# Softmax denominators of a head pair: four products of 32 array columns instead of four of 64, with small VectorE copies behind them

## The reference, cut to what matters

```python
q, k, v = tanh(states @ Wq + bq), tanh(states @ Wk + bk), tanh(states @ Wv + bv)   # 16 heads x 64
alpha = einsum('bhqd,bhkd->bhqk', q, k) / sqrt(64)
alpha = where(causal, alpha, finfo.min)
alpha = softmax(alpha, axis=-1)
ctx   = einsum('bhqk,bhkd->bhqd', alpha, v)
return tanh(ctx @ Wo + bo)
```

## Time and profile before

| | before |
|---|---|
| median of 3 runs | 1678.64 us (1678.16 to 1680.62) |
| span of the profiled execution | 1681.5 us |
| PE busy | 1618.6 us (96%) |
| DVE busy | 1440.7 us (86%) |
| ACT busy | 1208.0 us (72%) |
| POOL busy | 460.7 us (27%) |
| chain that ended last | PE 85%, DVE 8%, ACT 3%, issue 2%, POOL 1% |
| line 608 in that chain | 3% |
| granted PE clock over the span | 0.989 |

### The profile page before, as it was taken

One profiled execution on the slowest core, in us unless ns is written; L12 is line 12 of the kernel. 1 busy time (PEld: TensorE's weight loads), 2 busy tenths in 40 slices (PEclk: granted clock), 3 DMA queues, 4 the chain that ended last, 5 costly groups with the idle time before them and its releaser, 6 DMA issues.

```text
span 1681.5 us, 38177 instructions
## 1 busy us (share of the span) xinstructions
PE 1618.6 (96%) x14842; PEld 712.2 (42%) x14842; DVE 1440.7 (86%) x2099; ACT 1208.0 (72%) x1208; POOL 460.7 (27%) x563
## 2 busy tenths in 40 slices
PE   7899999999999999998999999999999999989996
PEld 3444444444444444444233333333332332456774
DVE  6877777888888888996999999999999999488888
ACT  5666766666667666654887888788878888775776
POOL 4211112333332323341234232323332332220004
PEclk9999999999999999997999999999999999999998
DMA  5311111011110110011012000200030000000001
GB/s 142 72 39 37 37 37 39 20 37 37 37 37 36 37 37 21 22 32 32 14 39 51 9 12 16 48 12 13 16 74 20 13 16 21 1 8 8 14 13 50
DMA packets 46602, 52.94 MB, mean 31 GB/s; under 512 B 9279, under 2 KB 33551, under 8 KB 46482
## 3 DMA queue, kind: packets, MB, share of 16 engines
q1 hardware_dynamic: 45584, 50.05, 10.2%
q10 hardware_dynamic: 898, 1.22, 0.3%
HBM read 15.07 MB, written 10.49 MB: 15 GB/s over the span
## 4 chain that ended last, share of the span: by engine, by line
PE 85%; DVE 8%; ACT 3%; issue 2%; POOL 1%; ACTq 0%; POOLq 0%; DVEq 0%
PE psum L1872 15%; PE psum L590 15%; PE psum L571 11%; PE psum L1857 9%; PE psum L1883 7%; PE psum L533 5%; PE psum L1503 4%; PE psum L1470 4%; PE psum L608 3%; DVE arena L2333 3%; PE psum L628 2%; PE psum L553 1%; ACT arena L2101 1%; PE psum L554 1%; PE psum L555 1%
## 5 line engine op out<-in xcount | busy, mean ns | idle before, releaser
L2333 DVE TENSOR_REDUCE arena<-psum 128x2 f32<-128x1024 f32 x490 | 585.4, 1219 | 39.2 <-PE psum L1883 33.0
L2101 ACT ACTIVATE arena<-psum 128x1024 f32<-128x1024 f32 x512 | 524.2, 1026 | 131.6 <-PE psum L1857 117.9
L755 ACT ACTIVATE arena<-psum 128x2048 f32<-128x2048 f32 (+1 forms) x160 | 274.0, 1713 | 229.0 <-PE psum L571 228.9
L1872 PE MATMUL psum<-arena 128*32 128x256 f32 x4096 | 327.8, 392 | 0.7
L859 POOL TENSOR_SCALAR_AFFINE_SELECT arena<-arena 128x512 f32<-128x512 f32 (+1 forms) x160 | 152.5, 971 | 508.9 <-ACT arena L755 508.9
L590 PE MATMUL psum<-arena,hs 128*64 128x512 f32 (+3 forms) x1536 | 283.0, 496 | 0.2 <-POOL arena L859 0.2
L571 PE MATMUL psum<-arena 64*128 64x512 f16 (+3 forms) x2304 | 215.0, 324 | 2.1 <-DVE arena L907 1.6
L1857 PE MATMUL psum<-arena 32*128 32x512 bf16 x1024 | 198.9, 385 | 3.7 <-DVE arena L2333 3.0
L1883 PE MATMUL psum<-arena 32*128 32x512 bf16 x980 | 189.0, 382 | 6.0 <-ACT arena L2101 2.4
L907 DVE TENSOR_TENSOR arena<-arena 128x1024 f16<-128x1024 f32 x64 | 78.4, 1226 | 101.5 <-ACT arena L734 101.5
L590 PEld LDWEIGHTS psum<-arena,hs 128*64 128x64 f32 x1536 | 96.0, 136 | 141.5 <-issue 125.2
(11 more groups left out here) (221 smaller groups left out, 2127.5 us busy)
## 6 DMA issues: line engine op xcount, KB each, us to landing
arena<-arena SPq DMA_DIRECT2D x30, 512.0 KB, 2.9
arena<-arena SPq DMA_DIRECT2D x46, 128.0 KB, 2.2
arena<-latent_q SPq DMA_DIRECT2D x64, 64.0 KB, 2.0
arena<-latent_k SPq DMA_DIRECT2D x64, 64.0 KB, 2.0
arena<-arena SPq DMA_DIRECT2D x60, 64.0 KB, 2.3
X<-in_L_attn_states SPq DMA_DIRECT2D x4, 512.0 KB, 4.6
latent_q<-arena SPq DMA_DIRECT2D x16, 96.0 KB, 2.2
latent_k<-arena SPq DMA_DIRECT2D x16, 96.0 KB, 2.3
```

Of the source, the lines that this page charges most:

```text
L755: nc.scalar.activation(probs[g], SC[:, :, 0:WIDTH[g]], ACT.Exp, scale=DH ** -0.5).then_inc(exp_done, 1)
L1872: last = nc.tensor.matmul(OT[ROWS * c:ROWS * (c + 1), h * HALF // 2:(h + 1) * HALF // 2], v_cols[par][:, kt, 2 * pr + i, :], e_probs[u % 4 ...
L2101: nc.scalar.activation(e_probs[u % 4], src, ACT.Exp, scale=KD ** -0.5).then_inc(e_done, 1)
L2333: nc.vector.tensor_reduce(half_tops[:, kh, qt, 2 * pr:2 * pr + 2], src.rearrange("p (i c) -> p i c", i=2), AX.X, ALU.max).then_inc(top_don ...
```

## The change

The four products of a pair now have 32 columns of ones each and go to four groups of 32 rows of one PSUM bank: row group c holds head c // 2 and half c % 2 of the queries. They raise `den_done` once, by 2. DVE transposes that one bank with one instruction; `denT` has 512 words instead of 1024. The reciprocal reads the 16 numbers of each partition twice and writes 32. Four new copies (`share`), each of 32 partitions by 16 numbers, take the inverses of a row group to the neighbouring row group of the same head, so that all 64 rows of a head hold both halves; then `spread` is as before. `share` stands where `spread` stood, between the first and the second `hi_third`, and `spread` moves behind the second. In the tail `share` stands directly ahead of `spread`.

```diff
-        denT = a1b.take(S)
+        denT = a1b.take(HALF)
...
+        QB = HALF // 32
+        INVERSE = 6
...
-                for half in range(2):
-                    now = slice(half * HALF, (half + 1) * HALF)
-                    for s in range(2):
-                        last = nc.tensor.matmul(PJ[s * DH:(s + 1) * DH, now], ones, sums[par][:, s, now],
-                                                start=True, stop=True, skip_group_check=True)
-                    last.then_inc(den_done, 1)
+                for c in range(4):
+                    s, half = c // 2, c % 2
+                    last = nc.tensor.matmul(PJ[ROWS * c:ROWS * (c + 1), 0:HALF], ones[:, 0:ROWS],
+                                            sums[par][:, s, half * HALF:(half + 1) * HALF],
+                                            start=True, stop=True, skip_group_check=True)
+                last.then_inc(den_done, 2)
...
-                for half in range(2):
-                    dve.wait_ge(den_done, 2 * n + half + 1)
-                    now = slice(half * HALF, (half + 1) * HALF)
-                    nc.vector.transpose(denT[:, now], PJ[:, now]).then_inc(den_read, 1)
+                dve.wait_ge(den_done, 2 * n + 2)
+                nc.vector.transpose(denT, PJ[:, 0:HALF]).then_inc(den_read, 2)
...
-                nc.vector.reciprocal(rden_col, denT.rearrange("p (b c) -> p b c", c=32)[:, :, 0]).then_inc(rden_ready, 1)
+                v = denT.rearrange("p (b c) -> p b c", c=32)[:, :, 0].unsqueeze(1).to_broadcast([P, 2, QB])
+                nc.vector.reciprocal(rden_col.rearrange("p (h b) -> p h b", h=2), v).then_inc(rden_ready, 1)
+
+            def share(n):
+
+                dve.wait_ge(rden_ready, INVERSE * n + 1)
+                for c in range(4):
+                    half, other = c % 2, c ^ 1
+                    now = slice(half * QB, (half + 1) * QB)
+                    nc.vector.tensor_copy(rden_col[ROWS * other:ROWS * (other + 1), now], rden_col[ROWS * c:ROWS * (c + 1), now]
+                                          ).then_inc(rden_ready, 1)
...
                 hi_third(i, par, 0)
                 if at_least(i, 1):
+                    share(i - 1)
+                hi_third(i, par, 1)
+                if at_least(i, 1):
                     spread(i - 1)
-                hi_third(i, par, 1)
                 hi_third(i, par, 2)
```

## The result

| | before | changed |
|---|---|---|
| median, same chip, 4 runs each | 1678.46 us (1678.16 to 1680.62) | 1697.57 us (1697.40 to 1697.97) |
| ratio, 95% interval | | 1.0100 (1.0082 to 1.0117) |
| span of the profiled execution | 1681.5 us | 1696.1 us |
| granted PE clock over the span | 0.989 | 0.986 |
| chain that ended last | PE 85%, DVE 8%, issue 2% | PE 72%, DVE 13%, issue 9% |

The account below looks back on a forecast made before the run. PE and DVE's chain were taken to set the pace together, with POOL's selects limiting PE. Terms +8.8 (21 late pairs), -1.9 (pairs 2 to 9), +0.4 (pair 1) and +0.1 gave +7.4, 1686.0 us; range 1674 to 1690.

Parts of the forecast that it names:

- PE's block: Denominator products on PE: two rounds 0.92 us plus 0.20 for arrangement changes, 1.12 instead of 1.82, saving 0.70.
- Rival 3: PE alone counts: its 0.70 us arrives in full in 31 pairs, -22 us, 1656.6 us; chance 0.02.
- rival 4: The four products don't run side by side: block 1.92 us, PE +0.1 a pair, 1686 to 1690 us; chance 0.03.
- Rival 2: One charge absent: copies one at a time but unblocked by the select, or flowing but blocked; 1675.6 us; chance 0.31.
- Rival 1: Copies cheap, 0.36 us for four, and the select lets them pass; about 11 us faster, 1667.6 us; chance 0.08.
- pair 14's kind: Pairs 10 to 27 and 28 to 30, closing on DVE's chain: +0.42 us each, +8.8 us over 21 pairs.
- (a): DVE's transposes of the denominators: one goes, -0.60 us in pair 14 and -0.74 in pair 7.
- Step (e): Second and third `hi_third` on DVE, now with the transpose between them: -0.10 us.
- the 0.68: Four DVE copies that change rows, each beginning when the one before has ended; part of 2.20 us from first to second `hi_third`.
- the charge of the select: First DVE copy waits for POOL's select of group 4: 0.31 to 0.48 us, taken as 0.36.
- Pair 7's kind: Pairs 2 to 9, where PE itself is last before the values: -0.24 us each, -1.9 us over eight.
- the last pair and the product behind the loop: End of the loop, where DVE waits for the products too: +0.1 us.

Follow-up runs that it names:

- the narrow products alone: Changed kernel with PE's four 32-column products, but two DVE transposes of the one bank, the old order and no copies; 1676.75 us, ratio 0.9987 to the kernel before.
- the short select: Changed kernel with POOL's select of group 4 cut from 128 columns to 8; 1685.88 us, ratio 1.0022 to the kernel before.

## Why the prediction was wrong

**Right: the mechanism of the pairs and its place.** PE's block (1.00 us and 0.10 ahead of it, against 1.12), PE waiting ahead of context 3 and ahead of the values, DVE's chain setting the late pairs, copies one at a time, a select blocking the first: each is in the rows, and each was taken away by itself, with the pairs going where the mechanism says. Rival 3 is refuted by the narrow products alone, rival 4 by the block of 1.00 us. Rival 2 needed one of the two charges to be absent; they are there with 0.49 (row changes) and 0.32 us (select). Rival 1 needed both to be absent. No kernel here has the copies on DVE with both charges gone; with the copies gone altogether a late pair gains 22.43 - 22.16 = 0.27, where rival 1 had 0.3.

**Off by 3 us: sizes.** In pair 14's kind the transpose gives the -0.60 of (a): 367.89 - 366.88 = 1.01 to the first `hi_third`, where it was 365.95 - 364.34 = 1.61. Step (e) gives its -0.10: from the second `hi_third` to line 922 it is 372.53 - 370.19 = 2.34, against 1.15 for the transpose and 369.47 - 368.18 = 1.29. The mis-sized term is the middle one, 2.30 instead of 2.20, because each held instruction (four copies and the `hi_third` behind them) starts some 0.03 us after the end of the one before it, which the 0.68 left out; the charge of the select, 0.32 for 0.36, gives a part of that back. So +0.52 by these rows and +0.51 by the windows, not +0.42. Pair 7's kind gained 0.06 instead of 0.24: the same 0.10, and the transpose starts 0.14 us behind the end of the products (206.50 + 1.07), so that step (a) gives -0.62, not -0.74. DVE and PE there:

```profile
207.71 0.72 DVE L927 STREAM_TRANSPOSE arena<-psum 128x512 f32<-128x512 f32 x1 [0.16 <-PE psum L609]
...
213.37 1.21 DVE L922 TENSOR_TENSOR acc<-psum,acc 128x1024 f32<-128x1024 f32 x1
```
```profile
214.63 0.23 PE L555 MATMUL psum<-arena 128*128 128x128 f16 x1 [0.37 <-DVE acc L922]
```

Over the program: pairs 10 to 30 +10.3, not +8.8; pairs 1 to 9 +0.2, not -1.9 and +0.4; the lead, where no instruction changed, +0.7; and about -1.0 behind the loop at the high clock. That makes the +10.2 of equal clocks out of the forecast's +7.4. The lead up to the first pair lasts between 24.5 and 26.1 us over the kernels of this study; what sets it is open.

**The failed step: "the last pair and the product behind the loop ... +0.1 by the same terms".** The terms were DVE's and PE's durations at full clock. At full clock they were nearly right: in the execution with the high clock the changed kernel is 11.2 us behind ahead of the last pair and 11.1 at the start of the last denominators. They put the clock at nothing without a reason: that PE has two long waits there, that the clock stood at half behind both, and that the change lengthens both. The low clock cost 1.6 us in this very stretch and 9.4 in all, 3.4 times the error in all other terms together (2.8). The same blindness is in the base line. The trace of the kernel before already had its clock at half in this place:

```profile
783.00:790.00 7.00, 7.00 (x34) 4.49 (x31) 2.62 (x8) 2.05 (x2) 0.00 (x0) 0.50 0.29 61
```

The profile's 0.989 stood in the table of before, and read as "2.9 above the median" it hid that this kernel has executions with and without 5 us of low clock. The range up to 1690 contained the kernel at the high clock (1688.54) and nothing else of it.

**Open.** Waits of 1.98 and 3.24 us were followed by 23.9 us at half clock in one execution and by full clock, but for a few us, in the next. That filling PE's waits makes the low clock rarer is shown for the changed kernel (four of four runs at 0.991 to 0.994, against one of eight above 0.989 without) and for the one with the copies on ACT (0.991 to 0.993, against 0.987 to 0.990). That the length of the waits orders the kernels is not shown: with the copies on ACT the waits are 1.17 and 2.31 us, nearly those of the kernel before, and none of nine runs was above 0.990, while 36 of 55 runs of the kernel before were; with the short select they are 1.66 and 3.23, and three of ten runs reached 0.992 or 0.993. What decides in a single execution is open too.

## What to carry to other kernels

- Taking work from an engine pays only as far as the next edge of that place. Find for each kind of stage who ends the engine's wait and how far the next one is behind: here that is some 0.5 us in the early pairs, where the selects come next, and in 21 others the next edge, DVE's chain, is already reached.
- A small instruction is not priced by its elements. Four copies of 16 numbers take 1.1 us of DVE's chain because they change rows and stand beside a select; the same copies on an engine with idle time cost the pairs nothing.
- Where a change lengthens PE's waits at a place that already has long ones, give the clock a term of its own, and before using a profile as base line see which clock it ran at beside several runs.

## What was unexpected of the hardware

- An instruction of 32 rows by 16 numbers lasts 168 ns on DVE and 202 ns on ACT; on DVE the next starts 0.077 us behind it when rows stay and 0.20 us when they change.
- A DVE copy of 16 numbers that meets a POOL select doesn't slip in: it ends right behind the select (364.93 against 364.90). The Trainium skill has the port that the two share as a lock that is held for a whole instruction and never split (SBUF — State Buffer, Terms, at the shared port pair); this trace agrees, with 486 ns for the first copy of a late pair and 172 at most once the select is short.
- The same program ran at 0.986 and at 0.995 of the clock, 1699.48 and 1688.54 us: a spread of 0.65%, larger than the effect of most edits tried here. Its two profiled executions have the same waits to 0.01 us and are 9.4 us apart.
- Four float32 products of 32 columns (512 moving) take PE 1.00 us, and the change of form costs 0.10 us more ahead of them (1.87 against 1.77 us for the block in front).
